# The first dense layer of a recommender kernel in three float32r passes of split operands, and the embedding chunk's transpose moved behind the residual

## The reference

```python
embed_x = emb_table[X + offsets[None, :]]            # 2048 x 39 x 64
att = embed_x
for i in range(3):                                   # 2 heads of 32
    att = relu(softmax(q k^T) v + att @ WR[i])       # q, k, v = att @ WQ, WK, WV
att_output = relu(att.reshape(B, 2496) @ Wlin)
h = relu(embed_x.reshape(B, 2496) @ W1 + b1)         # 2496 x 512
h = relu(h @ W2 + b2)                                # 512 x 256
dnn_output = relu(h @ W3 + b3)
return sigmoid(att_output + dnn_output)
```

## Time and profile before

| | |
|---|---|
| median of 3 runs | 2049.63 us (2048.24 to 2055.91) |
| the profiled execution | 2049.93 us, span 2048.0 us |
| TensorE, matmuls busy | 1954.7 us (95%) |
| TensorE, weight loads busy | 1612.0 us (79%) |
| VectorE busy | 1614.2 us (79%) |
| ScalarE busy | 1289.5 us (63%) |
| GpSimd busy | 860.0 us (42%) |
| mean granted TensorE clock | 0.994 of full speed |
| DMA, mean over the span | 32 GB/s |

### The profile page before, as it was taken

The page is one execution under the profiler, slowest core; times in us unless marked ns, Lnnn a source line. Parts: engine busy times, 40 slices in busy tenths (PEclk is TensorE's granted clock), DMA queues, the critical chain, the costliest instruction groups (busy, mean ns, idle before and its releaser), DMA issues.

```text
span 2048.0 us, 103306 instructions
## 1 busy us (share of the span) xinstructions
PE 1954.7 (95%) x44640; PEld 1612.0 (79%) x44640; DVE 1614.2 (79%) x3429; ACT 1289.5 (63%) x3269; POOL 860.0 (42%) x949
## 2 busy tenths in 40 slices
PE   1598999999999999999999999999999999999998
PEld 0377888887888888888888888888888888887887
DVE  2376778887787888878788787888888788887887
ACT  0265666666666666666666666666666666666665
POOL 6544354444444444454444434444443444443000
PEclk9999999999999999999999999999999999999999
DMA  4111111111111111111111111111111111111000
GB/s 151 23 28 25 31 27 32 29 30 31 27 33 27 31 29 30 31 29 31 29 30 29 28 33 27 32 29 30 31 27 33 27 32 28 30 30 26 21 19 17
DMA packets 67561, 64.61 MB, mean 32 GB/s; under 512 B 23768, under 2 KB 54504, under 8 KB 67112
## 3 DMA queue, kind: packets, MB, share of 16 engines
q1 hardware_dynamic: 47144, 37.52, 6.2%
q0 software_dynamic: 19968, 20.49, 5.1%
HBM read 27.24 MB, written 0.01 MB: 13 GB/s over the span
## 4 chain that ended last, share of the span: by engine, by line
PE 94%; another core or an unknown queue 2%; issue 1%; DVE 1%; POOL 1%; SPq 1%; ACT 0%; DMA 0%; ACTq 0%
PE SV L445 21%; PE Ob L462 14%; PE Mb L400 13%; PE X L430 13%; PE X L423 9%; PE X L425 5%; PE X L424 5%; PE Ob L423 3%; PE Ob L424 3%; PE Ob L425 3%; PE Ob L391 2%; PE Mb L416 1%; POOL emb L324 1%; PE Mb L411 0%
## 5 line engine op out<-in xcount | busy, mean ns | idle before, releaser
L324 POOL DMA_INDIRECT emb<-L_rec_emb_table,idx_t x624 | 630.1, 1010 | 792.4 <-PE Ob L462 615.1
L666 DVE TENSOR_REDUCE den<-pe_sb 103x16 f32<-103x624 f32 x384 | 308.5, 803 | 316.3 <-ACT pe_sb L561 311.5
L445 PE MATMUL SV<-yv,xs 64*39 64x142 f32 x12288 | 455.0, 286 | 11.6 <-ACT v_sb L563 10.9
L445 PEld LDWEIGHTS SV<-yv,xs 64*39 64x39 f32 x12288 | 345.2, 113 | 53.0 <-issue 14.1
L545 ACT ACTIVATE xs<-Ob 128x312 f32<-128x312 f32 x256 | 110.6, 432 | 388.2 <-PE Ob L462 388.2
L648 DVE TENSOR_REDUCE mx<-SV 103x8 f32<-103x312 f32 x768 | 332.7, 474 | 26.9 <-PE SV L445 20.4
L462 PEld LDWEIGHTS Ob<-pt,v_sb 39*32 39x32 f32 x12288 | 273.2, 106 | 92.8 <-issue 91.8
L430 PE MATMUL X<-ident,pn 103*103 103x103 f32 x3072 | 341.8, 254 | 0.0
L572 ACT COPY pt<-X 103x312 f32<-103x312 f32 x768 | 284.8, 424 | 78.6 <-PE X L430 39.1
L400 PE MATMUL Mb<-w,embT 128*128 128x512 f32 (+1 forms) x640 | 331.7, 599 | 0.9 <-ACT embT L518 0.7
L462 PE MATMUL Ob<-pt,v_sb 39*32 39x39 f32 x12288 | 324.1, 198 | 7.8 <-issue 6.6
(11 more groups left out here) (71 smaller groups left out, 2336.6 us busy)
## 6 DMA issues: line engine op xcount, KB each, us to landing
v_x<-v_sb SPq DMA_DIRECT2D x768, 39.0 KB
emb<-L_rec_emb_table,idx_t POOLq DMA_INDIRECT x624
w<-L_rec_W SPq DMA_DIRECT2D x1, 4864.0 KB
w<-L_rec_W SPq DMA_DIRECT2D x1, 512.0 KB
idx_in<-r_X SPq DMA_DIRECT2D x1, 312.0 KB, 3.9
b_b<-L_rec_b SPq DMA_DIRECT2D x1, 256.0 KB
w<-L_rec_W SPq DMA_DIRECT2D x1, 128.0 KB
b_b<-L_rec_b SPq DMA_DIRECT2D x1, 128.0 KB
```

The lines of the kernel that those rows point to most:

```text
L324: nc.gpsimd.indirect_dma_start(out=emb[:, n % ER, f % 2 * D:(f % 2 + 1) * D], out_offset=None, in_=table, in_offset=bass.IndirectOffsetOnA ...
L445: last = nc.tensor.matmul(SV[64 * b:64 * b + F, at:at + YR], x_pair(u, e, p), yv[64 * e:64 * e + D, l, p, :], start=True, stop=True, skip_ ...
L666: nc.vector.tensor_reduce(den[:], pe_sb[:], AX.X, ALU.add).then_inc(den_ready, 1)
```

## The change

1. **First layer split.** W1 is kept as two float32r tensors, `w1_hi` and `w1_lo` (W1 minus its high half), and each transposed chunk is split in the same way into `c_hi` and `c_lo` (three buffers each). The one fp32 matmul of a chunk becomes three float32r matmuls: `c_lo` by `w1_hi`, `c_hi` by `w1_lo`, `c_hi` by `w1_hi`. All three take 128 rows; the last chunk's missing 64 rows of `w1_hi` and `w1_lo` are zero.
2. **Conversions in the steps.** ScalarE makes `c_hi` at the end of its step, VectorE `c_lo` behind the low half of x. In step `ts` they convert chunk `ts + 3`; TensorE uses it two steps later.
3. **Conversions at the start.** W1 arrives in 20 pieces of at most 256 KB through four staging buffers, behind the other weights; from the fifth piece on SyncE waits until VectorE has finished with the buffer. ScalarE and VectorE split four pieces ahead of each block of tile 0's chunks. TensorE waits for all of W1 only before its first first-layer matmul, no longer before its first transpose.
4. **Room in SBUF.** `xs` has two buffers instead of three (layers 1 and 2 share one), the weighted outputs go into the second of them instead of `prod` and W1 is staged there too, and exp is written over its input. The ReLU of layer 0 now waits for the sums of the tile before, and those sums run in steps 0 to 7 of a tile instead of 4 to 11.
5. **The transpose moved.** TensorE transposes the embedding chunk behind the residual product, ahead of the transposes of pn, instead of ahead of the residual. With a residual in front it no longer starts an accumulation of its own (`start=alone`).

The diff, cut to its core:

```diff
@@ constants
+    CONVERT_AHEAD = 2
+    CR = 3
+    WS = 4
-    SUM_AT = 4
+    SUM_AT = 0
@@ buffers
-        w1 = sb("w1", [128, FC, N1])
+        w1_hi = sb("w1_hi", [128, FC, N1], F32R)
+        w1_lo = sb("w1_lo", [128, FC, N1], F32R)
+        c_hi = sb("c_hi", [128, CR, TB], F32R)
+        c_lo = sb("c_lo", [128, CR, TB], F32R)
-        xs = sb("xs", [128, L, XC])
-        prod = sb("prod", [128, UL, C])
+        xs = sb("xs", [128, 2, XC])
+        w1_in = xs[:, 1, 0:WS * N1].rearrange("q (s n) -> q s n", n=N1)
-        pe_sb = sb("pe_sb", [KR, G, H, F])
+        pe_sb = sd
@@ which chunk is converted in a step
+        def converted_at(s):
+
+            t, n = tile_step(s + CONVERT_AHEAD + 1)
+            return (t, n) if n < FC and t < TILES else None
@@ SyncE
-            sp.dma_start(w1[:, 0:FC - 1, :],
-                         W1[0:(FC - 1) * 128, :].rearrange("(c p) n -> p c n", p=128)).then_inc(ld_d, 16)
-            sp.dma_start(w1[0:LASTW, FC - 1, :], W1[(FC - 1) * 128:, :]).then_inc(ld_d, 16)
...
+            for n in range(FC):
+                w = LASTW if n == FC - 1 else 128
+                at_least(sp, w1_lo_ready, n - WS + 1)
+                sp.dma_start(w1_in[0:w, n % WS, :], W1[n * 128:n * 128 + w, :]).then_inc(ld_w1[n % WS], 16)
@@ TensorE
             def first_layer(t, n):
 
-                w = LASTW if n == FC - 1 else 128
-                if t > 0:
-                    pe.wait_ge(embT_ready, chunk_count(t, n))
+                i = t * FC + n
+                pe.wait_ge(c_lo_ready, i + 1)
                 if n == 0:
                     at_least(pe, h2_ready, t)
-                return nc.tensor.matmul(Mb[:], embT[0:w, t % 2, n, :], w1[0:w, n, :], start=(n == 0), stop=(n == FC - 1))
+                nc.tensor.matmul(Mb[:], c_lo[:, i % CR, :], w1_hi[:, n, :], start=(n == 0), stop=False)
+                nc.tensor.matmul(Mb[:], c_hi[:, i % CR, :], w1_lo[:, n, :], start=False, stop=False)
+                return nc.tensor.matmul(Mb[:], c_hi[:, i % CR, :], w1_hi[:, n, :], start=False, stop=(n == FC - 1))
...
             for k in range(NB):
                 first_embedding(k)
             pe.wait_ge(first_embT, NB)
+            pe.wait_ge(w1_lo_ready, FC)
             first_layer(0, 0)
...
-                if chunk_at(s):
-                    embedding(*chunk_at(s))
                 if 0 <= u < TOTAL:
                     if chunk_at(s - 1):
                         pe.wait_ge(embT_ready, chunk_count(*chunk_at(s - 1)))
                     product(Ob[:, 0:C], layer_of(u), 256, u % XS)
+                if chunk_at(s):
+                    embedding(*chunk_at(s), u < 0)
+                if 0 <= u < TOTAL:
                     pe.wait_ge(pn_ready, u + 1)
@@ ScalarE
+            def convert_high(t, n):
+
+                i = t * FC + n
+                w = LASTW if n == FC - 1 else 128
+                chunk_embedded(act, t, n)
+                if i >= CR:
+                    at_least(act, o_ps, (i - CR) // FC * NU + (i - CR) % FC - PV_AT)
+                    act.wait_ge(c_lo_ready, i - CR + 1)
+                nc.scalar.copy(c_hi[0:w, i % CR, :], embT[0:w, t % 2, n, :]).then_inc(c_hi_ready, 1)
...
             for k in range(NB):
+                for n in range(k * BK, (k + 1) * BK):
+                    w = LASTW if n == FC - 1 else 128
+                    act.wait_ge(ld_w1[n % WS], 16 * (n // WS + 1))
+                    nc.scalar.copy(w1_hi[0:w, n, :], w1_in[0:w, n % WS, :]).then_inc(w1_hi_ready, 1)
                 first_embedding(k)
...
+                    if layer_of(u) == 0:
+                        at_least(act, lin_sum, (u // NU - 1) * UL + u % UL + 1)
...
+                if converted_at(s):
+                    convert_high(*converted_at(s))
@@ VectorE
+            def convert_low(t, n):
+
+                i = t * FC + n
+                w = LASTW if n == FC - 1 else 128
+                dve.wait_ge(c_hi_ready, i + 1)
+                nc.vector.tensor_tensor(c_lo[0:w, i % CR, :], embT[0:w, t % 2, n, :], c_hi[0:w, i % CR, :],
+                                        ALU.subtract).then_inc(c_lo_ready, 1)
...
                 if s + LEAD < TOTAL:
                     split_low(s + LEAD)
+                if converted_at(s):
+                    convert_low(*converted_at(s))
```

More of the change, by code:

```diff
@@ L177, in autoint @@
         weights_ready = sem("weights_ready")
+        ld_w1 = [sem(f"ld_w1_{k}") for k in range(WS)]
+        w1_hi_ready = sem("w1_hi_ready")
+        w1_lo_ready = sem("w1_lo_ready")
+        c_hi_ready = sem("c_hi_ready")
+        c_lo_ready = sem("c_lo_ready")
         idx_ready = sem("idx_ready")
@@ L383, in first_embedding, with embedding @@
                 last.then_inc(first_tr_ps, 1)
-            def embedding(t, n):
+            def embedding(t, n, alone):
                 w = LASTW if n == FC - 1 else 128
@@ L606, in split_low @@
                 dve.wait_ge(xh_ready, u + 1)
-                nc.vector.tensor_tensor(x_lo[:, u % XS, :], xs[:, layer_of(u), layer_cols(u)], x_hi[:, u % XS, :],
+                nc.vector.tensor_tensor(x_lo[:, u % XS, :], xs[:, x_buffer(layer_of(u)), layer_cols(u)], x_hi[:, u % XS, :],
                                         ALU.subtract).then_inc(xl_ready, 1)
-            for k in range(NB):
+            def convert_low(t, n):
[4 more added lines that the diff above has]
+                                        ALU.subtract).then_inc(c_lo_ready, 1)
+            for k in range(NB):
+                for n in range(k * BK, (k + 1) * BK):
+                    w = LASTW if n == FC - 1 else 128
+                    dve.wait_ge(w1_hi_ready, n + 1)
+                    nc.vector.tensor_tensor(w1_lo[0:w, n, :], w1_in[0:w, n % WS, :], w1_hi[0:w, n, :],
+                                            ALU.subtract).then_inc(w1_lo_ready, 1)
                 dve.wait_ge(first_embT, k + 1)
+                if k == 0:
+                    for n in range(CONVERT_AHEAD + 1):
+                        convert_low(0, n)
                 for e in range(2):
@@ L622, in weighted @@
                     dve.wait_ge(embT_ready, chunk_count(*chunk_at(u + PV_AT)))
-                at_least(dve, lin_sum, last_outputs(u) - UL)
-                nc.vector.scalar_tensor_tensor(out=prod[:, u % UL, :].rearrange("q (p f) -> q p f", f=F),
+                nc.vector.scalar_tensor_tensor(out=weighted_outputs(u),
                                                in0=Ob[:, 0:C].rearrange("q (p f) -> q p f", f=F), scalar=0.0,
```

27 lines of the change are left out of this document (21 added, 6 removed).

## The result

The changed kernel takes 2034.61 us (median of 5 runs, 2030.98 to 2038.03), the kernel before 2050.53 in the same comparison: a ratio of 0.9917, 95% interval 0.9898 to 0.9936. It is faster by 0.8%, not by the forecast 3.5%; 2034.61 lies outside the range of 1962 to 2000. Of 71 us, 16 came.

A forecast was written before the change was run, and what follows sets the result against it. TensorE was taken to bound the kernel, each nanosecond saved there counting in full. Gains of 54 + 3 + 6 + 9 = 72 us, less about 1, took 2049.9 to 1979 us; range 1962 to 2000.

The forecast's parts named there:

- The passes: First layer: three float32r passes of 0.23 us replace 0.86 us per chunk, saving 0.17 us in 320 chunks, 54 us.
- B: First layer: a pass costs half an fp32 record, gaining 69 us instead of 54, time 1964 us; chance 0.10.
- D: First layer: weight loads stand open, each chunk takes 0.16 us more, time 2084 us; chance 0.04.
- The last chunk: The 64-row chunk: padding to 128 rows removes its extra 0.19 us, 16 times, 3 us (0 to 5).
- The transpose moved: Chunk's transpose behind the residual costs 0.02 us less in each of 300 chunks, 6 us.
- Conversions added: Chunk conversions, 83 us of ScalarE and 90 us of VectorE, fit into idle time and cost nothing.
- Rival C: Scores wait for ScalarE's v_sb copy; with half the steps' gain lost, time 2009 us; chance 0.08.
- The sums' move: VectorE's linear-part sums move to steps 0 to 7; in steps 0 and 1, 0.67 us just fits into 0.75.
- Before the first step: At the start, with less W1 in flight, GpSimd's whole 8.94 us standstill goes, gaining 9 us.
- Rival A: The start does not gain but loses 3 us, time 1991 us; chance 0.17.
- Rival E: GpSimd's copies hold up VectorE's c_lo at a shared SBUF port, 24 us at most, showing as 1990 us; chance 0.03.

The follow-up runs named there:

- b_high_late: Kernel before with one edit: ScalarE's rounding of x moved behind its copy to v_sb; 2007.16 us, 0.9965 of the kernel before.
- e2_high_late: Changed kernel with ScalarE's rounding of x moved behind its copy to v_sb; 1971.55 us, 0.9782 of the kernel before.
- e3_no_conversion: Changed kernel without the in-step conversions of chunks to c_hi and c_lo (300 of each); 1990.3 us, 0.9877 of the kernel before.
- r_after: Changed kernel, unedited, measured again on a chip of the faster kind; 1988.18 us, 0.9853 of the kernel before.
- h1_quarter: Changed kernel with VectorE adding b1 to only 128 of 512 columns; 1984.89 us, 0.9849 of the kernel before.
- r_before: Kernel before, unchanged, measured again on a chip of the faster kind; 2016.93 us, 0.9999 of itself.
- r2_after: Changed kernel, unedited, measured again on a chip of the slower kind; 2036.76 us, 0.9926 of the kernel before.

## Why the prediction was wrong

The time missed the forecast by 58 us on the profiled spans (13 of 71). The steps of the prediction that failed, by size: the first layer's 0.17 us a chunk was put into the sum in full, and a step got 0.11 (some 20 us, with the transposition); step 9 was not priced (13); the standstill at the start did not go (11); steps 18 and 19 were not priced (6).

**The passes.** Right as a price: 0.23 us each, 0.69 for 0.86, no weight load open, so rivals B (0.215) and D (over 0.28) are out. Wrong as a term of the sum, by "a nanosecond taken from TensorE in a step is a nanosecond of the time": 0.17 us at the first layer was not 0.17 us in a step. In steps that wait for no other engine (b_high_late against e2_high_late, steps 5 to 8) the scores start at 3.02 in place of 3.18, and the step takes 4.90 in place of 5.01. The missing 0.05 us goes in the weighted values, whose 32 matmuls take 0.64 to 0.65 us from the first start to the last in place of 0.60. What lengthens them is not known; the profile names no wait. 320 x 0.11 are 35 of the 54 us.

**The last chunk.** Right: step 18 lost 0.40 us, 5.32 to 4.92, where 0.17 for the passes and 0.19 for the padding were forecast. But step 19 grew by 0.48 (see below).

**The transpose moved.** Wrong: 6 us forecast, none measured. I read 0.11 us off for the place in front and took 0.09 for the place behind from the transposes of pn; both places cost 0.115. The difference of 0.02 lay below what one step's rows can give.

**Conversions added.** That they cost nothing held for the total (e3_no_conversion), though not for the gathers of step 9. What came after it, "what becomes late next is the scores' wait for v_sb ... Of these 0.38 us the change takes 0.19", did not. From v_sb's end to the scores' start 0.14 us pass even when nothing else is waited for (r_after, steps 4 to 9; the "issue" piece above), so the margin was 0.24, and still it should have held. What broke it is a second form of the loop. These rows are one turn in the changed kernel, in order of time:

```profile
1006.53 0.41 PE L457 MATMUL X<-x_lo,w_hi 128*128 128x312 f32 x1
1006.75 0.86 DVE L727 TENSOR_TENSOR sd<-SV,mx 103x312 f32<-103x312 f32 x2
1006.84 0.43 ACT L600 ACTIVATE xs<-Ob 128x312 f32<-128x312 f32 x1 [1.44 <-PE Ob L496]
...
1008.91 0.60 ACT L618 COPY v_sb<-SV 103x512 f32<-103x512 f32 x1
...
1009.66 1.18 PE L479 MATMUL SV<-yv,xs 64*39 64x142 f32 x32
...
1011.79 0.43 ACT L600 ACTIVATE xs<-Ob 128x312 f32<-128x312 f32 x1 [1.44 <-PE Ob L496]
```

From ReLU to v_sb's end 2.67 us, 0.15 to the scores, 2.13 to the next ReLU: 4.95 us. The ReLU starts 0.31 us after the step's X product here. In the kernel before it started 0.13 us after it (X product 1002.81, ReLU 1002.94) and ran the same 2.68 us to v_sb. With the early ReLU the loop is 0.18 us shorter, 4.77 us, and lies under TensorE's 4.90; with the late one it is 4.95 and above it. In the kernel before TensorE's 5.01 us lay above both. The change took TensorE's step below the longer form, and the loop paces the steps that fall into it. ScalarE stands 1.44 us in each of these steps, waiting for the weighted values: idle time that is part of a closed loop and no slack. I counted it as cover. But this error of mechanism does not account for the missing time: the edit that shortens the loop gives 9 to 10 us in the chunk steps of the changed kernel, and 14 in those of the kernel before.

**Rival C** names this mechanism and gave it 0.08 and half of the steps' gain. The mechanism is there, in 123 of the 252 chunk steps of r_after, and not by a VectorE crowded in steps 0 and 1, where nothing is late. The price is not: about half of the steps' gain is indeed missing, but the kernel before had as much to win from the late rounding, so it is not shown to be the loop's. That C's half comes near is luck.

**The sums' move and steps 18 and 19.** I checked the crowded steps 0 and 1, which held, and not the one in which VectorE also adds b1. Before, TensorE's longer step 18 hid that chain; now it lengthens step 19, as h1_quarter shows: the two steps together took 10.11 us before and 10.19 after. The forecast had 0.38 + 0.02 off them in each tile, some 5 us.

**Before the first step.** Wrong: "The whole standstill goes: 9 us". The stand of 8.94 us stayed with W1 gone (9.19) and shrank with W1 in place on another chip (2.19). I inferred a cause from 2 us between two ends. What the engines stand for until 34 us on the first kind stays open. **Rival A**, with its +3 us end, came true: +2.3. The forecast named the conversions of W1 for it. TensorE's third block of transposes does wait 4.20 us for ScalarE's evacuation, which now stands between blocks of W1; that these waits make the 2.3 us was not tried.

**Rival E.** GpSimd's copies did lengthen, 752 to 826 ns, and by e3_no_conversion (760) it is the conversions that do it. The 20 us do not lie on the chain, but GpSimd's next gathers come later for it: this was not in my rival. The Trainium skill (SBUF — State Buffer, two separate sides) has VectorE and GpSimd lock each other out of a port pair; the 760 and 818 ns agree with it, though no run here tells such a lock from another hindrance.

**Step 9** I did not see at all: 10 us on the first kind, 5 on the second, from a standstill that the profile charges to nothing. In the first pair of traces TensorE's gaps there add up to 5.4 us before and 15.3 after, which is the whole difference.

The account of the first pair of traces, in us saved; what the forecast had is worked out from its own terms:

| | forecast | measured |
|---|---|---|
| 252 chunk steps | 48 | 27 |
| step 9 | 3 | -10 |
| steps 18 and 19 | 5 | -1 |
| start | 9 | -2 |
| steps 20 to 22, tiles 0 and 15, tail | 6 | 0 |
| together | 71 | 13 |

Of the 21 us that the chunk steps lack, by the pair with the late rounding, 0.02 us a step (5) is the transposition and 0.06 (15) the first layer's gain that does not arrive.

## What to carry to other kernels

Look for closed loops before counting an engine's idle time as slack: add up the way from one engine through the others and back, in its longest observed form, and compare that with the bound engine's step; it caps the gain at the moment the bound engine drops below it. But an edit that gains in the changed kernel shows what could be won there and not what the change lost: try the same edit in the kernel before, and compare step by step, since in the totals another step hid half of it. When a step is shortened, the steps that differ from the common one (here those with an extra VectorE operation, or with late gathers) have to be costed one by one. A cause read off from two events near each other in time ("the load ends, then the engine goes on") is worth its chance only, and a second trace of the same kernel on another chip is the cheapest test of it.

## What was not expected of the hardware

**Two chips, one program.** The same kernel took 2016 or 2051 us. Most of the difference is in the first 220 us: standstills of all engines at fixed places (the changed kernel's tile 0 took 147.6 us and 123.9 us). The clock adds to it: in the kernel before no matmul starts from 80 to 88 us, and the granted clock is 0.66 there, 0.70 from 88 to 96 and 0.91 from 160 to 200; in r_before, without that stand, it is 1.00 in all three. The kernel's own gain differed too, 0.9917 and 0.9926 against 0.9853.

**ReLU late behind VectorE.** Of 224 ReLUs in tiles 1 to 14 of r_before, 209 start 0.22 to 0.31 us after the start of the last weighted-values matmul and 12 start 0.37 to 0.51 after it; in r_after 58 and 152. In 138 of these 152 VectorE's subtraction sd, which reads PSUM as the ReLU does, starts 0.25 to 0.4 us after that matmul, mostly 0.1 before the ReLU (in the rows above 1006.75 and 1006.84); in none of the 58 early ones does it start so late. Since sd's time follows the scores' and the scores' follow v_sb, lateness keeps itself up. That the two reads hinder each other is only argued.

**A long gather late in a step.** In fourteen traces of the changed kernel and its variants that have such gathers, every one that GpSimd issued between 2.3 and 4.9 us into a step and that took over 1.3 us goes with a gap of TensorE in the weighted values: 12 of 12 in r2_after, 1.2 us each, 11 of 11 in r_after, 0.47 us each. Of the long ones issued earlier (72 in r_after) none does, and of the short late ones 1 of 80. The kernel before had no long one there in its two traces, but on the first kind 11 of its short late ones go with a gap, and b_high_late has 14 gaps beside short ones, so the length is not a condition. What stops TensorE isn't known.
